# A graph network kernel: the weighted identities of rounds k = 1 to 4 made by ScalarE instead of VectorE

## The chip, the cores and the metric

The kernel runs on one core of a Trainium2 chip. The metric is the device time of one launch in microseconds (us), of which three runs are given as a median. The engines are called PE (TensorE, the matrix engine), DVE (VectorE), ACT (ScalarE), POOL (GpSimd) and SP (SyncE, which only issues transfers here).

## The reference

Four graph blocks follow one another on a table x of 50,000 nodes by 128 features, with 25,000 edges sorted by their target (dst). Each block's result is added to x and the sum is layer-normalised. All the change's work lies in the second block (L1):

```python
def prop(z):
    return jax.ops.segment_sum(edge_weight[:, None] * z[src], dst, num_segments=N_SUP)
for i in range(L):                       # L = 5 layers
    z = h @ W[i] + b[i]
    x_start = prop(z)
    xi = h
    for _ in range(RHP):                 # RHP = 5 rounds
        xi = (prop(xi) + x_start) / (2.0 + GAMA)
    mean = jnp.mean(xi, axis=0)
    var = jnp.var(xi, axis=0)
    out = gamma[i] * (xi - mean) / jnp.sqrt(var + BN_EPS) + beta[i]
    h = jnp.where(out > 0, out, LEAKY_SLOPE * out)
return h[seg_ids]
```

`prop` gathers the row of each edge's source, multiplies it by the edge's weight and adds up the rows that have one target. In this network all seg_ids are 0, so h is the same row everywhere before the first layer.

## The kernel before, in words

**Layout.** The 25,000 edges lie in T = 200 tiles of 125 edges (TE). A tile occupies 128 partitions. GR = 4 tiles are a group, so a round has GPR = 50 groups. Tables of edge rows live in HBM (`tabs`, three of them); a round reads one and writes another.

**Layers and rounds.** Layer l = 0 of block L1 is done in closed form (`scalars_*`). Layers l = 1 to 4 are a hardware loop, and in each of them the rounds k = 0 to 4 are written out (NL = 5), so k = 1 to 4 occur 16 times in all, with 800 groups. A round on each engine:

- POOL, `l1_gather` (line 1018): 200 indirect transfers, one per tile, each of 128 rows of 128 floats into ring G of 20 tiles (five groups). Before the first it waits until all stores of the round before have landed (`l_tab`), and before every second group until PE has read an old group (`l_ft`).
- PE, `forward` (line 1347, k >= 1): for each tile the matmul of the gathered tile with a diagonal matrix, the identity scaled by the tile's 128 edge weights. That turns the tile to features x edges and weights it in one step, into a PSUM bank (`FT_`). It waits for the scan two groups back (`l_sc`), for the four diagonal matrices (`l_dg`), and for each tile's landing (`l_got`). `backward` (line 1372) turns a scanned group back to edges x features. PE runs forward of group n+1, then backward of group n (`lagged`).
- DVE, `scanned` (line 1410): the running sum along the edges, cut where the target changes (`keyrow` is 0 there); it reads PSUM and `keyrow`. Behind it `scaled_identity` (line 1382) makes the four diagonal matrices of the next group, as one product of 128 x 512 elements of `ident` and `wz` (both in SBUF) into a half of M. In k = 1 to 3 `rows_out` (line 1434) then adds the constant part and writes Y. In k = 4 (`last`) two other instructions follow the diagonal matrices: a masked product (line 1422, of `keyrow` and the scan, both in SBUF) and batch statistics (line 1425).
- ACT has nothing in k = 1 to 3. In k = 4 `kept_act` copies the scan of a group (`copied`, line 1326), then the turned-back rows of the group before it from PSUM to Y (`rows_out`, line 1333). In k = 0 it has two activations a group (lines 1313 and 1317).
- SP stores Y of each group to the table (line 995).

The order on each engine is written out by hand; semaphores (counts that start at 2 by `credit`, so that `g + 1` means "group g - 2 is done" and `g + 3` means "group g is done") tie the engines together. M has two halves of four matrices, `h = q % 2`, so the matrices of group n overwrite those of group n - 2. In `lagged` the first function runs one group ahead of the second.

```python
            if k:
                scaled_identity(0, 0)
            else:
                leaky_nodes(0, 0)
            lagged(dve, scanned, (lambda i, q: None) if last else rows_out)
```

Of the kernel before, what the change touches and what calls it, by code (L numbers as in the profile page):

```python
# [5 lines left out]
ALU, ACT, AX = mybir.AluOpType, mybir.ActivationFunctionType, mybir.AxisListType  # L6

P, D = 128, 128
# [3 lines left out]
GR = 4  # L12
# [5 lines left out]
NB = 10  # L18
# [3 lines left out]
NL = 5  # L22
# [13 lines left out]
def build(nc, x0, src, dst, ea, ew, w0, b0, w1, b1, gamma, beta, w2, b2, we, be, coef, linw, linb, asrc, adst, out):  # L36
# [31 lines left out]
    with ctx:  # L68
# [20 lines left out]
        ident = sb("ident", [P, P])  # L89
# [15 lines left out]
        wz = sb("wz", [P, TP])  # L105
# [11 lines left out]
        M = sb("M", [P, U, P])  # L117
# [39 lines left out]
        def steady(eng, *values):  # L157


            for v in values:  # L160
                if not isinstance(v, int):
                    eng.lower_val(v)
            eng.wait_ge(s_go, 1)
# [787 lines left out]
        def every_group(eng):  # L951

            with eng.Fori(0, NI) as i:
                for q in range(NB):
                    yield i, q

        def lagged(eng, one, two):

            one(0, 0)
            with eng.Fori(0, NI - 1) as i:  # L960
                for q in range(NB):
                    one(i + (q + 1) // NB, (q + 1) % NB)
                    two(i, q)
            for q in range(NB):
                if q < NB - 1:
                    one(NI - 1, q + 1)
                two(NI - 1, q)

        def group_no(l, k, i, q):

            return round_of(l, k) * GPR + NB * i + q
# [5 lines left out]
        def is_last(i, q):  # L977

            return isinstance(i, int) and i == NI - 1 and q == NB - 1
# [322 lines left out]
        def scalars_act(act):  # L1302
            for g in range(GPR):
                act.wait_ge(o_ex, g + 1)
                nc.scalar.copy(zt_at(GR * g), bank(g % 2)).then_inc(l_xc, 1)

        def turned_act(act, l):

            for i, q in every_group(act):
                h, n, g = q % 2, (l - 1) * GPR + NB * i + q, group_no(l, 0, i, q)  # L1310
                steady(act, n + 1, g + 3, g + 1)
                act.wait_ge(l_z, n + 1)
                nc.scalar.activation(HTR[h][:].rearrange("p s f -> p (s f)"), zt_at((NB * i + q) * GR), ACT.Identity,
                                     bias=tcol[:, 0:1], scale=scol[:, 0:1]).then_inc(l_hc, 1)
                act.wait_ge(l_ft, g + 3)
                act.wait_ge(l_sc, g + 1)
                nc.scalar.activation(M[:, GR * h:GR * h + GR, :], PS[:, FT_[h], :, :], ACT.Identity,  # L1317
                                     bias=tcol[:, 0:1], scale=scol[:, 0:1]).then_inc(l_he, 1)

        def kept_act(act, l):  # L1320

            def copied(i, q):
                g = group_no(l, NL - 1, i, q)
                steady(act, g + 3)
                act.wait_ge(l_sc, g + 3)
                nc.scalar.copy(zt_at((NB * i + q) * GR), S[q % 2]).then_inc(l_zc, 1)  # L1326

            def rows_out(i, q):
                g, before = group_no(l, NL - 1, i, q), 16 * stores_before(l, NL - 1, i, q)
                steady(act, g + 3, before)  # L1330
                act.wait_ge(l_bk, g + 3)
                act.wait_ge(l_tab[q % NG], before)
                nc.scalar.copy(group_of(Y, q % NG), PS[:, BK_[q % 2], :, :]).then_inc(l_ev, 1)
            lagged(act, copied, rows_out)

        def l1_pe(pe, l, k):

# [38 lines left out]
        def l1_dve(dve, l, k):  # L1376
            last = k == NL - 1

            def scaled_identity(i, q):
                h = q % 2  # L1380
                dve.wait_ge(l_ft, group_no(l, k, i, q) + 1)
                nc.vector.tensor_tensor(M[:, GR * h:GR * h + GR, :], ident[:].unsqueeze(1).to_broadcast([P, GR, P]),  # L1382
                                        wz[:, bass.ds((NB * i + q) * GR, GR)].unsqueeze(2).to_broadcast([P, GR, P]),
                                        ALU.mult).then_inc(l_dg, 1)

            def leaky_nodes(i, q):
                u, n = HTR[q % 2][:].rearrange("p s f -> p (s f)"), (l - 1) * GPR + NB * i + q
                dve.wait_ge(l_hc, n + 1)
                nc.vector.scalar_tensor_tensor(u, u, 0.01, u, ALU.mult, ALU.max).then_inc(l_hl, 1)

            def scanned(i, q):
                h, g, tile = q % 2, group_no(l, k, i, q), (NB * i + q) * GR
                n = (l - 1) * GPR + NB * i + q
                half = M[:, GR * h:GR * h + GR, :].rearrange("p s f -> p (s f)")
                if k == 0:
                    dve.wait_ge(l_he, n + 1)
                    nc.vector.scalar_tensor_tensor(half, half, 0.01, half, ALU.mult, ALU.max).then_inc(l_lr, 1)
                    if not is_last(i, q):
                        leaky_nodes(i + (q + 1) // NB, (q + 1) % NB)
                    dve.wait_ge(l_lr, n + 1)  # L1400
                    dve.wait_ge(l_wc[q % NG], 32 * (NB // NG * NI * (l - 1) + NB // NG * i + q // NG + 1))
                    nc.vector.tensor_tensor(half, half, WR[:, q % NG, :], ALU.mult).then_inc(l_mu, 1)
                    dve.wait_ge(l_mu, n + 1)
                else:
                    dve.wait_ge(l_ft, g + 3)
                dve.wait_ge(l_bk, g + 1)
                dve.wait_ge(l_sc, g + 2)
                if last:
                    dve.wait_ge(l_zc, n + 1)
                nc.vector.tensor_tensor_scan(S[h], keyrow[:, bass.ds(tile * P, GR * P)],  # L1410
                                             half if k == 0 else bank(FT_[h]), S[1 - h][:, GR * P - 1:GR * P],
                                             ALU.mult, ALU.add).then_inc(l_sc, 1)
                if k == 0:
                    dve.wait_ge(l_z, n + 3)
                    nc.vector.tensor_tensor(zt_at(tile).rearrange("p (s f) -> p s f", f=D), PS[:, ZB_[h], :, :],
                                            wide(bias, P, GR), ALU.add).then_inc(l_za, 1)
                elif not is_last(i, q):
                    scaled_identity(i + (q + 1) // NB, (q + 1) % NB)
                if last:
                    dve.wait_ge(l_sc, g + 3)  # L1420
                    mk = HTR[h][:].rearrange("p s f -> p (s f)")
                    nc.vector.scalar_tensor_tensor(mk, keyrow[:, bass.ds(tile * P + 1, GR * P)], 1.0, S[h],
                                                   ALU.subtract, ALU.mult).then_inc(l_mk, 1)
                    dve.wait_ge(l_mk, n + 1)
                    nc.vector.bn_stats(stL[:, bass.ds(NB * i + q, 1), :].rearrange("p a b -> p (a b)"),
                                       mk).then_inc(l_bn, 1)

            def rows_out(i, q):
                h, g = q % 2, group_no(l, k, i, q)
                dve.wait_ge(l_bk, g + 3)  # L1430
                if k == 0:
                    dve.wait_ge(l_za, (l - 1) * GPR + NB * i + q + 3)
                dve.wait_ge(l_tab[q % NG], 16 * stores_before(l, k, i, q))
                nc.vector.tensor_tensor(group_of(Y, q % NG), PS[:, BK_[h], :, :],  # L1434
                                        zt_at((NB * i + q) * GR).rearrange("p (s f) -> p s f", f=D),
                                        ALU.add).then_inc(l_ev, 1)

            if k:
                scaled_identity(0, 0)
            else:  # L1440
                leaky_nodes(0, 0)
            lagged(dve, scanned, (lambda i, q: None) if last else rows_out)

# [45 lines left out]
        with nc.Block() as block:  # L1489
# [89 lines left out]
            @block.scalar  # L1579
            def _(act):  # L1580
                def layer(l):
                    if isinstance(l, int):
                        scalars_act(act)
                        return
                    steady(act, NCOEF * l)
                    act.wait_ge(l_col, NCOEF * l)
                    turned_act(act, l)
                    kept_act(act, l)
                over_layers(act, layer)
                act.wait_ge(l_col, NCOEF * NL)  # L1590
                act.wait_ge(l_fin, 1)
                nc.scalar.activation(HT[:, 0, :], PS[:, ZB_[0], 0, :], ACT.Identity, bias=tcol[:, 0:1],
                                     scale=scol[:, 0:1]).then_inc(l_rb, 1)
# [824 lines left out]
```

## Time and profile before

| | us |
|---|---|
| runs shown | 9612.27 (median; 9603.39 to 9615.67) |
| the profiled execution, its own time | 9691.98 |
| its span in the profile | 9690.2 |
| POOL busy | 6759.2 (70%) |
| PE busy | 5711.1 (59%) |
| DVE busy | 5407.2 (56%) |
| ACT busy | 1448.9 (15%) |

How to read it: a busy share is an average over stages, and the kernel's stages have different limits. The stretch in which rounds k = 1 to 4 lie begins 2059 us after the span's start and ends at 7254 us. Within it the engines wait for each other group by group, so what counts is which of them sets the pace of a group. Instructions that only wait, branch, set registers or issue transfers are not busy time; of an indirect transfer on POOL the busy time is that of making it ready, not of moving the data. The granted share of PE's full clock is 0.627 over the execution.

### The profile page before, as it was taken

The page shows a single profiled execution, that of the slowest core. Times are in us where ns is not written, and L with a number is a line of the kernel's source. Part 1 is how long each engine was busy: PE and PEld are TensorE (multiplying, and loading weights), DVE is VectorE, ACT ScalarE, POOL GpSimd, SP SyncE. Part 2 cuts the span into 40 slices and gives each one's busy share as a digit, 9 for nine tenths or more (in the row PEclk, how much of TensorE's full clock was granted, in tenths as well). Part 3 has the DMA queues.
Part 4 walks back from the last instruction along what each step waited for, and adds up shares of the span by engine and source line. Part 5 has one row for each costly group of instructions (what it writes and reads, how often), then busy time and mean ns, then how long its engine had stood idle before and what let it go on. Part 6 is the DMA issues. An engine that isn't in the chain of part 4 may idle for free. (4 is left out here: it accounts for less than half of the span.)

```text
span 9690.2 us, 103316 instructions
## 1 busy us (share of the span) xinstructions
PE 5711.1 (59%) x24229; PEld 4276.2 (44%) x24229; DVE 5407.2 (56%) x12873; ACT 1448.9 (15%) x3028; POOL 6759.2 (70%) x6509
## 2 busy tenths in 40 slices
PE   4646557766666766666666666666661775630191
PEld 2436224544444544444545445544440664530170
DVE  5668764554445754456744457644457774530277
ACT  0115000210002200012200012100026113430006
POOL 4767663577777777777777777777776776767566
PEclk8765776775555855556855557755555888865555
DMA  3137101577555765656678656668766227961107
GB/s 144 43 101 245 25 3 36 118 111 99 98 98 103 132 104 98 98 98 112 124 99 101 99 97 124 113 98 96 99 99 232 63 68 149 183 115 28 20 31 323
DMA packets 564282, 1024.03 MB, mean 106 GB/s; under 512 B 192219, under 2 KB 275724, under 8 KB 563556
## 3 DMA queue, kind: packets, MB, share of 16 engines
q0 software_dynamic: 192032, 330.29, 32.3%
q1 hardware_dynamic: 354372, 588.76, 20.1%
q10 hardware_dynamic: 17664, 102.61, 2.6%
q8 instruction: 75, 1.23, 0.1%
q14 instruction: 139, 1.14, 0.0%
HBM read 561.87 MB, written 471.67 MB: 107 GB/s over the span
## 5 line engine op out<-in xcount | busy, mean ns | idle before, releaser
L1018 POOL DMA_INDIRECT G<-tab,gidx x4000 | 4050.6, 1013 | 1625.4 <-issue 1406.8
L1347 PE MATMUL PS<-M,G 128*128 128x128 f32 x6400 | 2073.2, 468 | 1524.1 <-DVE M L1382 1011.7
L1347 PEld LDWEIGHTS PS<-M,G 128*128 128x128 f32 x6400 | 1504.5, 314 | 2175.3 <-DVE M L1382 917.5
L1410 DVE TENSOR_TENSOR_SCAN UO<-keyrow,UT,PS 128x512 f32<-128x512 f32 (+1 forms) x400 | 511.9, 1280 | 1112.9 <-PE PS L1347 1112.9
L1410 DVE TENSOR_TENSOR_SCAN UT<-keyrow,UO,PS 128x512 f32<-128x512 f32 (+1 forms) x400 | 512.0, 1280 | 1030.7 <-PE PS L1347 1030.7
L1326 ACT COPY big<-UO 128x512 f32 (+1 forms) x100 | 61.8, 618 | 3666.0 <-DVE UO L1410 3666.0
L1434 DVE TENSOR_TENSOR Y<-PS,big 128x512 f32<-128x512 f32 x800 | 546.0, 683 | 12.8 <-PE PS L1372 7.0
L1105 POOL DMA_INDIRECT Y<-pair_d,G x400 | 402.4, 1006 | 200.0 <-issue 130.8
L1382 DVE TENSOR_TENSOR M<-ident,wz 128x512 f32<-128x512 f32 x800 | 534.3, 668 | 0.0
L758 ACT ACTIVATE big<-big,nb,rs 128x128 f32<-128x128 f32 x1173 | 461.3, 480 | 428.0 <-POOL nb L749 357.7
L1372 PE MATMUL PS<-ident,UT 128*128 128x128 f32 x1600 | 422.8, 420 | 8.3 <-DVE UT L1410 8.3
L1372 PE MATMUL PS<-ident,UO 128*128 128x128 f32 x1600 | 423.6, 420 | 0.0
L1350 PE MATMUL PS<-ident,G 128*128 128x128 f32 x800 | 195.1, 310 | 364.9 <-DMA G<-tab,gidx 315.8
L1372 PEld LDWEIGHTS PS<-ident,UT 128*128 128x128 f32 x1600 | 343.2, 228 | 14.7 <-DVE UT L1410 14.7
L1257 PE MATMUL PS<-big 128*128 128x400 f32 x800 | 322.2, 529 | 44.0 <-DVE G L1151 26.8
L1372 PEld LDWEIGHTS PS<-ident,UO 128*128 128x128 f32 x1600 | 347.4, 230 | 0.0
L450 POOL DMA_INDIRECT G<-in_x,ridx x200 | 208.8, 1044 | 156.9 <-DVE ridx L520 95.2
L2260 PE MATMUL PS<-ident,cf 128*100 128x128 f32 x8 | 2.0, 426 | 526.6 <-DVE cf L2206 526.6
L2304 POOL DMA_INDIRECT agg<-Y,sidx x200 | 197.5, 988 | 153.5 <-DVE Y L2355 105.1
L902 POOL DMA_INDIRECT gidx<-lastpos,src_i x200 | 231.3, 1157 | 103.0 <-issue 68.0
L1350 PEld LDWEIGHTS PS<-ident,G 128*128 128x128 f32 x800 | 109.3, 148 | 431.6 <-DMA G<-tab,gidx 380.1
L1317 ACT ACTIVATE M<-PS,tcol,scol 128x512 f32<-128x512 f32 x200 | 155.4, 777 | 843.3 <-PE PS L1350 843.3
(500 smaller groups left out, 11436.0 us busy)
## 6 DMA issues: line engine op xcount, KB each, us to landing
tab<-Y SPq DMA_DIRECT2D x1050, 256.0 KB, 3.2
big<-agg SPq DMA_DIRECT2D x90, 832.0 KB, 12.6
G<-tab,gidx POOLq DMA_INDIRECT x4000, 4.1
WR<-w_d SPq DMA_DIRECT2D x200, 256.0 KB
big<-x SPq DMA_DIRECT2D x60, 832.0 KB, 4.9
xt_d<-big SPq DMA_DIRECT2D x30, 858.0 KB, 19.2
x2n<-big ACTq DMA_DIRECT2D x30, 838.5 KB, 3.5
big<-x2n SPq DMA_DIRECT2D x30, 838.5 KB, 12.6
```

The source lines that it names most:

```text
L450: pool.indirect_dma_start(G[:, j, 0:D], None, x0, bass.IndirectOffsetOnAxis(ap=ridx[:, j:j + 1], axis=0)).then_inc(a_got[j], 16)
L758: ins = nc.scalar.activation(X[0:np_, j, 0:D], V[0:np_, j, :], ACT.Identity, scale=rs[0:np_, s, j:j + 1], bias=nb[0:np_, s, j:j + 1])
L902: pool.indirect_dma_start(gidx[:, t:t + 1], None, lastpos, bass.IndirectOffsetOnAxis(ap=src_i[:, t:t + 1], axis=0)).then_inc(g_got, 16)
L1018: pool.indirect_dma_start(G[:, t % RG, 0:D], None, tab_in(k), bass.IndirectOffsetOnAxis(ap=gidx[:, t:t + 1], axis=0)).then_inc(l_got[t % R ...
L1105: pool.indirect_dma_start(GS[:, t, :], None, pair_d, bass.IndirectOffsetOnAxis(ap=G2[:, t:t + 1], axis=0)).then_inc(o_got, 16)
L1257: ins = nc.tensor.matmul(bank2(n % 2)[:, j, :], OH[:, 2 * n + j, :], CT, start=True, stop=True)
L1347: ins = nc.tensor.matmul(PS[:, FT_[h], j, :], G[:, s, 0:D], M[:, GR * h + j, :], start=True, stop=True)
L1350: ins = nc.tensor.transpose(PS[:, FT_[h], j, :], G[:, s, 0:D], ident[:])
L1372: ins = nc.tensor.transpose(PS[:, BK_[h], j, :], UR[h][:, j, :], ident[:])
L1382: nc.vector.tensor_tensor(M[:, GR * h:GR * h + GR, :], ident[:].unsqueeze(1).to_broadcast([P, GR, P]), wz[:, bass.ds((NB * i + q) * GR, GR ...
L1410: nc.vector.tensor_tensor_scan(S[h], keyrow[:, bass.ds(tile * P, GR * P)], half if k == 0 else bank(FT_[h]), S[1 - h][:, GR * P - 1:GR * P ...
L1434: nc.vector.tensor_tensor(group_of(Y, q % NG), PS[:, BK_[h], :, :], zt_at((NB * i + q) * GR).rearrange("p (s f) -> p s f", f=D), ALU.add). ...
```

## The change

ACT gets a function `scaled_identity`: it waits until PE has read the half of M (`l_ft`) and until the scan of two groups before is done (`l_sc`), then makes the four diagonal matrices with four activations (Copy, with the tile's column of `wz` as scale), the last of which raises `l_dg`. In rounds k = 1 to 3 ACT runs this for every group and nothing else. In k = 4 it runs it one group ahead of `copied` and `rows_out`, which now come as a pair. DVE's product and its wait are gone.

```diff
+        def scaled_identity(act, l, k, i, q):
+            h, g = q % 2, group_no(l, k, i, q)
+            steady(act, g + 1)
+            act.wait_ge(l_ft, g + 1)
+            act.wait_ge(l_sc, g + 1)
+            for j in range(GR):
+                ins = nc.scalar.activation(M[:, GR * h + j, :], ident[:], ACT.Copy,
+                                           scale=wz[:, bass.ds((NB * i + q) * GR + j, 1)])
+            ins.then_inc(l_dg, 1)
+
+        def weighted_act(act, l, k):
+            for i, q in every_group(act):
+                scaled_identity(act, l, k, i, q)
...
-            lagged(act, copied, rows_out)
+
+            def behind(i, q):
+                copied(i, q)
+                rows_out(i, q)
+            lagged(act, lambda i, q: scaled_identity(act, l, NL - 1, i, q), behind)
...
-            def scaled_identity(i, q):
-                h = q % 2
-                dve.wait_ge(l_ft, group_no(l, k, i, q) + 1)
-                nc.vector.tensor_tensor(M[:, GR * h:GR * h + GR, :], ident[:].unsqueeze(1).to_broadcast([P, GR, P]),
-                                        wz[:, bass.ds((NB * i + q) * GR, GR)].unsqueeze(2).to_broadcast([P, GR, P]),
-                                        ALU.mult).then_inc(l_dg, 1)
...
-                elif not is_last(i, q):
-                    scaled_identity(i + (q + 1) // NB, (q + 1) % NB)
...
-            if k:
-                scaled_identity(0, 0)
-            else:
+            if k == 0:
                 leaky_nodes(0, 0)
...
                     turned_act(act, l)
+                    for k in range(1, NL - 1):
+                        weighted_act(act, l, k)
                     kept_act(act, l)
```

## Rows read from the trace of the kernel before

**Rows 1.** Waits, rounds 1 to 3 of layer 2: us in total, times, longest us.

```profile
POOL G L1018 <- issue: 177.4, 582, 0.3
POOL G L1018 <- DMA tab<-Y: 33.3, 3, 13.7
POOL G L1018 <- PE PS L1347: 4.6, 15, 0.3
...
PE PS L1347 <- DVE M L1382: 185.8, 147, 2.2
PE PS L1347 <- DMA G<-tab,gidx: 86.6, 151, 6.6
```

**Rows 2.** The gathers of rounds 1 to 3: window, length, POOL busy (instructions), clock, DMA share, GB/s.

```profile
2061.90:2320.00 258.10, 196.06 (x200) 0.51 0.85 97
...
sum 3094.30, POOL 2340.28; mean POOL 195.02
```

**Rows 3.** The same for the gathers of round 4 of the four layers.

```profile
2863.80:3128.00 264.20, 201.44 (x200) 0.51 0.56 97
...
sum 1056.00, POOL 805.38; mean POOL 201.34
```

**Rows 4.** Two groups of round 3, layer 2: start us, length us, instruction.

```profile
4011.91 1.28 DVE L1410 TENSOR_TENSOR_SCAN UT<-keyrow,UO,PS 128x512 f32<-128x512 f32 x1 [2.86 <-PE PS L1347]
4012.11 0.96 POOL L1018 DMA_INDIRECT G<-tab,gidx  x1 [0.30 <-issue]
4013.11 0.67 DVE L1382 TENSOR_TENSOR M<-ident,wz 128x512 f32<-128x512 f32 x1
4013.37 1.23 POOL L1018 DMA_INDIRECT G<-tab,gidx  x1 [0.30 <-issue]
...
4018.33 0.68 DVE L1434 TENSOR_TENSOR Y<-PS,big 128x512 f32<-128x512 f32 x1
...
4018.68 0.95 POOL L1018 DMA_INDIRECT G<-tab,gidx  x1 [0.30 <-issue]
```

**Rows 5.** A group of round 4, layer 2: start us, length us, instruction.

```profile
4330.46 0.80 PE L1347 MATMUL PS<-M,G 128*128 128x128 f32 x2 [0.64 <-DMA G<-tab,gidx]
...
4331.05 1.06 PE L1372 MATMUL PS<-ident,UO 128*128 128x128 f32 x4
...
4332.68 0.67 DVE L1382 TENSOR_TENSOR M<-ident,wz 128x512 f32<-128x512 f32 x1
4332.96 0.62 ACT L1326 COPY big<-UT 128x512 f32 x1 [4.13 <-DVE UT L1410]
...
4333.40 1.65 PE L1347 MATMUL PS<-M,G 128*128 128x128 f32 x6 [1.29 <-DVE M L1382]
4333.48 0.58 ACT L1333 COPY Y<-PS 128x512 f32<-128x512 f32 x1
...
4338.06 0.68 DVE L1422 SCALAR_TENSOR_TENSOR OT<-keyrow,UO 128x512 f32<-128x512 f32 x1
...
4338.26 1.31 POOL L1018 DMA_INDIRECT G<-tab,gidx  x1 [0.30 <-issue]
```

**Rows 6.** The gathers and the products of line 1382: duration ns min/median/max.

```profile
L1018 POOL DMA_INDIRECT G<-tab,gidx x4000: 938/952/1879, 1760.3 to 7244.1; - x191
...
L1382 DVE TENSOR_TENSOR M<-ident,wz x800: 665/668/731, 2059.1 to 7246.0; 128x512 f32<-128x512 f32 x160
```

**Rows 7.** ACT by line and shape: count, busy us, mean ns of one.

```profile
L758 ACT ACTIVATE big<-big,nb,rs 128x128 f32<-128x128 f32 x1170 | 459.8, 480 | 425.9 <-POOL nb L749 357.7 <-DVE nb L779 26.1 <-issue 18.7
...
L2044 ACT COPY UO<-PS 128x128 f32<-128x128 f32 x30 | 8.0, 266 | 47.8 <-PE PS L2118 47.8
```

**Rows 8.** ACT's sequencer at line 1326: duration ns min/median/max.

```profile
L1326 ACTq FUSED_REGOPS  x160: 61/64/64, 2878.4 to 7202.8; - x160
```

**Rows 9.** The end of round 3, layer 2: backward and `rows_out` of its last group.

```profile
4228.99 1.11 PE L1372 MATMUL PS<-ident,UT 128*128 128x128 f32 x4 [0.52 <-DVE UT L1410]
...
4230.14 0.69 DVE L1434 TENSOR_TENSOR Y<-PS,big 128x512 f32<-128x512 f32 x1 [0.62 <-PE PS L1372]
```

## The prediction, as it stands on record

> **What bounds the kernel now.** I read three views in turn. The waits of POOL in rounds k = 1 to 3 say that it waits for nobody between gathers [rows 1]: 582 of its pauses are "issue", at 177.4 / 582 = 0.305 us each, only 15 are for PE (4.6 us in three rounds), and the only long ones are the three handovers to the next round. So in these rounds POOL is the engine that sets the pace: a gather's own time plus 0.30 us, four times a group. The windows give that time: 2340.28 us for 2400 gathers, 0.975 each [rows 2]. In round 4 it is 805.38 us for 800, 1.007 each [rows 3], a pace of 4 x (1.007 + 0.30) = 5.23 us a group.
>
> PE waits 185.8 us in these three rounds for the matrices M, which looks like the prize, and 86.6 us for gathers [rows 1]. It is none: a group's four tiles come at POOL's pace, and with M there sooner PE waits for the tiles instead.
>
> The third view is the timeline, and it shows why a gather costs more than the 0.95 that most of them take. The gather at 4013.37 began 0.26 us into DVE's product of line 1382, when 0.41 of it was left, and took 1.23. The one at 4018.68 began inside `rows_out` (line 1434), the one at 4012.11 inside the scan, and they took 0.95 and 0.96 [rows 4]. The scan and `rows_out` read one operand from PSUM, the product reads both from SBUF. In round 4 the masked product (line 1422), both operands in SBUF, does the same: a gather begun inside it took 1.31 [rows 5]. So **a DVE instruction with two SBUF inputs holds back a gather that begins inside it**. DVE itself is off the path: it waited 2.86 us for PE before that scan [rows 4].
>
> **The change part by part.**
>
> *Product gone, k = 1 to 3.* I take 0.948 for a gather that nothing holds up: the median of all 4000, held ones among them, is 0.952, the least 0.938 [rows 6], and most rows print 0.95. With 0.952 the next figure would be 55. 2340.28 - 2400 x 0.948 = 65 us are then stretch [rows 2], 65 / 12 = 5.4 us a round, and no other DVE instruction there has two SBUF inputs; the 800 products take 0.67 each, 0.73 at most [rows 6], so they are not held up in turn. POOL sets the pace, so all of it comes back: **-65 us**. As a check: a gather starts every 1.257 us, and one started with r us of the product left is late by about r - 0.13 (0.41 left, 0.28 late), which over a product of 0.67 us and any phase is 0.54 x 0.54 / 2 / 1.257 = 0.12 us a group, 6 us a round.
>
> *Product gone, k = 4.* The stretch is 805.38 - 800 x 0.948 = 47 us, 11.8 a round [rows 3], from the product and line 1422 together. Line 1422 stays, and moves up by 0.6 us to where the product stood, right behind the scan. There a two-input instruction costs 5.4 us a round, as in k = 1 to 3. So 47 - 4 x 5.4 = 25: **-25 us**. Bounds: 0.13 a group more or less from its phase; if line 1422 lost nothing at its new place, -47; if three quarters of the 47 are its own and stay, -12.
>
> *DVE's 0.67 us a group themselves* are worth nothing: after them DVE waits for PE, which waits for the gathers. At a round's end no product stands between the last group's scan, its backward and its `rows_out` [rows 9]: the last group issues none, by the code. So the handover stays as it is.
>
> *Four activations a group, k = 1 to 3.* The trace has no copy with one pointer operand. From below: a 128x128 COPY from PSUM takes 0.266 [rows 7]; 128x512 ones take 0.04 more from SBUF than from PSUM (0.62 and 0.58) [rows 5], so 0.30. From above: the ACTIVATE of line 758, 128x128 from SBUF with two pointers (scale and bias), takes 0.48, and 1170 of them in 459.8 us are 0.393 apart, so neighbours overlap by 0.09. I take the middle, 0.39, as this one has a single pointer: x = 3 x 0.30 + 0.39 = **1.29 us a group**, between 0.93 and 1.66. They can start when the scan two groups back is done, 1.4 us after that group's forward, and are needed when the forward one group on has ended, 5.1 us after it: some 3.7 us, on an engine that has nothing else. Cost zero; the cover would be gone only above that. Sequencer time, one register instruction of 0.064 each [rows 8], fits under an activation. Of transfers the change moves none.
>
> *Four activations a group, k = 4.* Here the order matters: ACT makes the matrices of group n+2 only after `rows_out` of group n, which waits for backward n, which stands on PE behind forward n+1. That closes a ring that was not there before: end of forward to end of backward 0.85 (4331.26 to 4332.11), to `rows_out` 0.05 (4230.10 to 4230.14) [rows 5, 9], its copy 0.58 less 0.10 of overlap (the copy before it starts 0.52 before it and lasts 0.62), the four activations x, to forward 0.05, and forward's eight passes: six take 1.65, two 0.80, so eight 2.08. Together 3.51 + x = **4.80 us**, against POOL's pace afterwards of 5.11 (5.23 less 25 / 200). It stays under it; cost zero, with 0.31 us a group in hand. `copied` moves behind the activations, but the scan that waits for it is two groups on.
>
> **Sum**: -65 - 25 = -90 us. The profiled execution has 9691.98 us, so 9602 for its like; it is 0.8% above the median run, and I carry the difference over unscaled: 9612.27 - 90 = **9522 us**.
>
> *A page's rule against the row.* The gather held up in the row was late by less than what was left of the product. The Trainium skill, page "SBUF — State Buffer", section "A bandwidth-pool intuition that's wrong (but worth ruling out)", has such a transfer blocked until the DVE instruction ends plus about 115 ns. By that rule each of 50 x 0.67 / 1.257 = 27 gathers a round would lose 0.335 + 0.115 on average, 12 us a round, and the change would give 16 x 12 = 192 us. The busy sums hold only 65 + 47, so the measurement decides.
>
> **The rivals.**
>
> *A. Round 4 turns onto ScalarE's ring (faster, but less).* With x above 1.60 the ring is longer than 5.11, and each 0.1 us costs 50 x 4 x 0.1 = 20 us. At the upper bound of 1.66 that is 12 us: 9534. At x = 1.92 (four at 0.48, no overlap) 64 us: 9586. For it: without overlap four of 0.39 take 1.56, right below the threshold. Against: line 758 shows the overlap [rows 7].
>
> *B. The same mechanism far enough to be slower.* It needs x above 2.145 to pass +19 us. One place: the activations of k = 4. If each takes the two-pointer price without overlap and its register instruction is not hidden, x = 4 x (0.48 + 0.064) = 2.18, the ring is 5.69, and -90 + 200 x (5.69 - 5.11) = +26: 9638. Of this the trace shows only the single prices. The Trainium skill, page "ScalarE: Activation LUTs", section "Rules for kernel authors", says to use VectorE, not ScalarE, for a multiplication; 1.29 against 0.67 us here agrees on the price, and whether it matters is what the ring decides.
>
> *C. No change.* The stretch would not come back: something else takes up POOL's 65 + 25 us, for instance the landings, for which PE waits 86.6 us [rows 1], because the gathers run at the memory's pace rather than POOL's. 9612. Against it: POOL's pauses are "issue" and not a full ring, and the transfer engines are 0.85 busy in one window shown and 0.56 in the other [rows 2, 3], with the gather's own time no longer in the first. That the change doesn't do what it says I exclude: nothing on DVE makes M afterwards.
>
> *D. The page's rule above*, 9420: no chance, since the sums bound it.
>
> **How the numbers follow.** A measurement of this kernel can tell some 0.2%, 19 us. Forecast 0.75; A at 9534 to 9590 0.08; C 0.10; B 0.07. Faster is 0.82 (forecast and nearly all of A), same 0.11, slower 0.07. The range: below, the whole stretch of both kinds gone, -112, gives 9500; above, the forecast's weak end (-55 by the floor of 0.952, -12 in round 4) is 9545, and I go on to 9590 to hold A and some of what lies toward C.
>
> **What would show it.** Right: the gathers' busy time in the windows of k = 1 to 3 falls to 190 us a round, with none above 1.0 us; in k = 4 to some 195, with the stretched ones all inside line 1422; ACT's four at 1.2 to 1.4 us a group; the pause for "issue" unchanged; PE's waits move from M to the gathers. Wrong: gathers still stretched where no two-SBUF instruction runs (C), or PE in k = 4 waiting for ACT's M and POOL for PE (A, B).

## The result, and the profile after

| | before | after |
|---|---|---|
| median of five runs, us | 9609.03 | 9562.54 |
| lowest and highest | 9603.39, 9615.67 | 9557.24, 9568.96 |
| the profiled execution, its own time | 9691.98 | 9559.96 |

The ratio is 0.9953 (95% interval 0.9942 to 0.9964): 46 us faster, where 90 were forecast. The sign and the range held; the size is half.

The busy times of the page after, and its costliest groups that the change touches:

```profile
PE 5802.3 (61%) x24229; PEld 4310.9 (45%) x24229; DVE 4949.1 (52%) x12073; ACT 2449.6 (26%) x6228; POOL 6656.3 (70%) x6509
...
L1018 POOL DMA_INDIRECT G<-tab,gidx x4000 | 3952.7, 988 | 1622.0 <-issue 1407.3
L1365 PE MATMUL PS<-M,G 128*128 128x128 f32 x6400 | 2226.2, 472 | 1344.2 <-DMA G<-tab,gidx 949.2
...
L1313 ACT ACTIVATE M<-ident,wz 128x128 f32<-128x128 f32 x3200 | 1021.4, 390 | 2382.4 <-DVE UO L1421 1238.9
```

The product's 534 us are gone from DVE, which waits longer for PE instead, and ACT's four activations a group take 1021 us. In k = 1 to 3 PE's waits moved from M to the gathers, as forecast. In k = 4 they did not: PE waits for M in nearly every group, now for ACT's. That is half of the forecast's sign of rival A. The other half, POOL waiting for PE, is absent (k = 4 of layer 2: us in total, times, longest us):

```profile
PE PS L1365 <- ACT M L1313: 93.4, 48, 2.2
...
POOL G L1018 <- PE PS L1365: 1.5, 5, 0.3
```

The windows of the gathers after, k = 1 to 3, answer to [rows 2] (first, last and sum of twelve):

```profile
2056.20:2314.00 257.80, 190.23 (x200) 0.52 0.82 100
...
6628.00:6884.00 256.00, 188.72 (x200) 0.51 0.63 101
sum 3081.50, POOL 2275.41; mean POOL 189.62
```

And k = 4, to [rows 3]:

```profile
2840.60:3100.00 259.40, 195.42 (x200) 0.53 0.50 99
...
sum 1035.20, POOL 779.18; mean POOL 194.80
```

2340.28 to 2275.41 is the forecast's 65 us to the microsecond, and 805.38 to 779.18 is 26 where 25 were forecast. Counted gather by gather, those begun inside the product lost 64.5 us in k = 1 to 3 of the kernel before, which is the whole stretch there; in the changed kernel no gather of k = 1 to 3 takes over 0.97 us, and all 78 stretched ones of k = 4 began inside the masked product.

Yet these 91 us of POOL time appeared as 46 in the timed runs. The two profiled executions, on the other hand, lie 132 us apart. Some 28 of those fall between the last rounds and the third scatter (indirect transfers to `agg`, one per tile), where the two kernels are the same: 1165 and 1137 us from the last transfer of the second scatter to the first of the third. So the profile of before was not an execution like the timed ones. That is the question that the experiments take up.

### The profile page after: what moved, and what is told of

The parts are those of the page before. It is cut to its first block and busy times, and to the rows that moved or that the text cites. A ratio compares the mean times of both kernels' runs of the same rounds, so it can differ in the third digit from the quotient of the medians.

```text
span 9558.2 us, 109668 instructions
## 1 busy us (share of the span) xinstructions
PE 5802.3 (61%) x24229; PEld 4310.9 (45%) x24229; DVE 4949.1 (52%) x12073; ACT 2449.6 (26%) x6228; POOL 6656.3 (70%) x6509
## 5 line engine op out<-in xcount | busy, mean ns | idle before, releaser
L1018 POOL DMA_INDIRECT G<-tab,gidx x4000 | 3952.7, 988 | 1622.0 <-issue 1407.3
L1365 PE MATMUL PS<-M,G 128*128 128x128 f32 x6400 | 2226.2, 472 | 1344.2 <-DMA G<-tab,gidx 949.2
L1365 PEld LDWEIGHTS PS<-M,G 128*128 128x128 f32 x6400 | 1539.3, 310 | 2052.8 <-DMA G<-tab,gidx 1463.8
L1313 ACT ACTIVATE M<-ident,wz 128x128 f32<-128x128 f32 x3200 | 1021.4, 390 | 2382.4 <-DVE UO L1421 1238.9
L1384 PE MATMUL PS<-cf 128*128 128x512 f32 x400 | 260.9, 741 | 8.3 <-DVE UT L1421 4.2
```

Source lines behind the costliest of these rows:

```text
L1018: pool.indirect_dma_start(G[:, t % RG, 0:D], None, tab_in(k), bass.IndirectOffsetOnAxis(ap=gidx[:, t:t + 1], axis=0)).then_inc(l_got[t % R ...
L1313: ins = nc.scalar.activation(M[:, GR * h + j, :], ident[:], ACT.Copy, scale=wz[:, bass.ds((NB * i + q) * GR + j, 1)])
L1365: ins = nc.tensor.matmul(PS[:, FT_[h], j, :], G[:, s, 0:D], M[:, GR * h + j, :], start=True, stop=True)
L1384: nc.tensor.matmul(bank(BK_[h]), QR[:, q % NG, :], BD, start=True, stop=False)
```

## The experiments

The runs were made in three jobs, and the record names another chip for each of them (9, 12 and 14). The kernel before ran in each as well, and its median differed: 9580.77, 9606.91 and 9687.95 us, so every figure below is read against its own job. It was profiled in job 1 only. "This chip" in an expectation written for job 2 means the chip of job 1, whose profiles it was worked out from.

| run | median us | ratio to before (95%) |
|---|---|---|
| job 1: before again | 9574.65 | 0.9993 (0.9984 to 1.0001) |
| ACT in k = 1 to 3 only | 9570.38 | 1.0001 (0.9979 to 1.0023) |
| identity in PSUM, product on DVE | 9561.89 | 0.9978 (0.9969 to 0.9987) |
| after again | 9542.95 | 0.9959 (0.9946 to 0.9972) |
| job 2: after, a spare product on DVE | 9621.35 | 1.0015 (1.0006 to 1.0024) |
| ACT in k = 4 only | 9581.27 | 0.9976 (0.9966 to 0.9985) |
| before, product 0.5 us later | 9794.91 | 1.0191 (1.0177 to 1.0205) |
| after, scan of k = 0 from PSUM | 9537.46 | 0.9927 (0.9914 to 0.9941) |
| job 3: after, ACT's part of k = 4 doubled | 9837.31 | 1.0142 (1.0123 to 1.0160) |
| after again | 9691.36 | 1.0002 (0.9992 to 1.0011) |
| after, scan of k = 0 from PSUM | 9689.70 | 1.0000 (0.9991 to 1.0010) |
| the same, masked product from PSUM too | 9719.86 | 1.0029 (1.0018 to 1.0041) |

### Before and after, profiled again in one job

No edit.

> The kernel before, unchanged, profiled again beside its own timed runs. The page that the forecast rested on was of an execution of 9692 us, while the timed runs have 9609. Theory (the stretch is in every execution, and the missing half of the gain is lost elsewhere): the gathers of k = 1 to 3 are busy 195 us a round again and those of k = 4 201 us, and the ratio is 1.000. Rival (that execution was a slow one, and its stretch was larger than the usual): the new profile has a span of about 9610 us, and the gathers' busy time is lower, so that the sum over the 16 rounds exceeds that of the changed kernel by about 50 us instead of 90.

> The changed kernel again, in the same job as the others. Both theories: 9562 within 5 us, ratio 0.995, gathers of k = 1 to 3 at 189.6 us a round with none above 1.0 us. It gives the profile that stands beside that of the kernel before from the same chip.

The changed kernel's ratio came as expected (0.9959), its median not (9543 for 9562), as the whole job was faster.

The windows of the gathers in k = 1 to 3 of layers 1 and 2, for the kernel before in this job (k = 1 of each layer, and the sum of the six; columns as in [rows 2]):

```profile
2058.90:2317.00 258.10, 192.74 (x200) 0.51 0.54 100
...
3419.20:3677.00 257.80, 192.84 (x200) 0.51 0.51 100
...
sum 1546.60, POOL 1153.54; mean POOL 192.26
```

And for the changed one (k = 2 of layer 1, and the sum):

```profile
2322.10:2580.00 257.90, 190.73 (x200) 0.50 0.54 101
...
sum 1545.30, POOL 1146.14; mean POOL 191.02
```

The rival was right: here the kernel before loses little to the stretch. Summed over all layers its gathers are busy 2301 us in k = 1 to 3 and 803 in k = 4, the changed kernel's 2281 and 779. That is 20 + 24 = 44 us, against 38 measured. The landings differ too. This is the time from issue to landing in k = 2 of layer 1 (min/median/max), first in the execution that the forecast used, then in this job's kernel before:

```profile
DMA to landing us min/median/max: 2.9/3.8/4.9
```

```profile
DMA to landing us min/median/max: 2.9/3.5/4.5
```

Over the whole kernel, for the gathers whose landing the trace shows, it is 4.1 us at the median and 13.4 at most in the forecast's execution, 3.5 and 7.2 here. What sets the stretch is the phase, that is, where the product stands against the gathers. Of the 600 products of k = 1 to 3, 18% here had a gather begin in their first 0.55 us, against 45% in the forecast's execution, about what a random phase gives (0.55 / 1.257 = 44%). A group's scan, and the product behind it, come after the landing of its last tile, so later or more scattered landings can move that phase. How much is due to which is argued and not shown: in the round above the landings are hardly more scattered, only 0.3 us later, and yet 23 of its 50 products met a gather in their first 0.55 us, against 12 of 50 here.

In k = 4 the masked product, one product later, meets the gathers in either case. It also carries most of the gain there: in this job it held gathers back by 36 us before and 18 after, while the product itself had cost 7. So 18 of the 25 us that k = 4 gave come from the masked product's new place right behind the scan, and not from the absence of the other.

### The same product with one operand in PSUM

```diff
-                nc.vector.tensor_tensor(M[:, GR * h:GR * h + GR, :], ident[:].unsqueeze(1).to_broadcast([P, GR, P]),
+                nc.vector.tensor_tensor(M[:, GR * h:GR * h + GR, :], PS[:, 6, 0, :].unsqueeze(1).to_broadcast([P, GR, P]),
...
+                        link(dve, "dve", nc.vector.tensor_copy(PS[:, 6, 0, :], ident[:]))
```

> The kernel before with one edit: DVE's product reads the identity from PSUM instead of SBUF, everything else stays on DVE. Theory (the two SBUF inputs are the cause): no gather of k = 1 to 3 is stretched, busy 190 us a round, and the gain is that of the full change or a little more, 40 to 60 us, 9550 to 9570, although DVE still spends its time. Rival (it is DVE's time, or M being late for PE, that the change takes away): no gain, 9609, or a slight loss, as the product becomes a little longer.

The identity is copied into PSUM once. It gained 19 us, where 40 to 60 were expected. Two rows of its timeline, a product and a gather that begins inside it:

```profile
3769.22 0.67 DVE L1382 TENSOR_TENSOR M<-PS,wz 128x512 f32<-128x512 f32 x1
...
3769.57 0.95 POOL L1018 DMA_INDIRECT G<-tab,gidx  x1 [0.30 <-issue]
```

Nothing is held, DVE spends the same 0.67 us, and k = 1 to 3 show the same busy time as the full change (191.01 a round in its six windows). So it is the operands and not DVE's time. It stays 19 us behind the full change: in k = 4 the masked product keeps its late place and most of its stretch (791 us against 779 over the four layers), which explains 12 of them. The other 7 stay open.

### One part alone

```diff
-                    for k in range(1, NL - 1):
-                        weighted_act(act, l, k)
```

This is the edit, against the changed kernel, for ACT in k = 4 only; DVE's product is put back in k = 1 to 3, and ACT's first group of k = 4 waits for the last forward of k = 3. For ACT in k = 1 to 3 only, the reverse.

> ACT makes the matrices in k = 1 to 3 alone, DVE again in k = 4. Theory (two SBUF inputs hold back a gather begun inside; the gain is spread over the rounds as the stretch is, 65 and 25 of 90): three quarters of the measured gain of 46 us, so some 35 us, 9574. Rival (k = 4 costs time by its ring through ACT, which eats the gain of k = 1 to 3): this kernel is faster than the full change, 9540 or less.

> ACT makes the matrices in k = 4 alone, DVE in k = 1 to 3. Theory: the gain here is what k = 4 lost of its stretch, 803 to 779 us over the four layers, so 20 to 25 us: 9556 to 9561, more than the k = 1 to 3 part gave on this chip (769 + 767 + 764 to 760 each, 20 us). Rival (the ring through ACT costs what the stretch gives back): 9581, with PE in k = 4 waiting for M and POOL for PE.

k = 4 alone gave 26 us, as expected and more than half of the change, though it is a quarter of the rounds. k = 1 to 3 alone gave 10 at the median, under the 35 expected, and its interval is so wide that it holds both 20 us and a loss: inconclusive by itself. Two of its twelve runs lie apart, at 9690 and 12369 us; the other ten have a mean of 9569. What its profile says is that the gathers of k = 1 to 3 are free again (759 us each over four layers) while those of k = 4 are held (801). Neither shows the ring to cost anything.

The profile of the kernel with ACT in k = 4 only tells of the product in job 2, where the kernel before took 9607 us, nearly the 9609 of the first timed runs. Its gathers of k = 1 to 3 are busy 2304 us, 29 above the 2275 of unheld ones. With some 24 in k = 4 (781 us there, and 805 in the next run) that makes 53 us on paper, near the 46 measured at first.

### A product that nobody needs

The changed kernel, and DVE multiplies the same two SBUF operands again behind each scan of k = 1 to 4, into an unused PSUM bank. It waits only for the one before it.

```diff
...
+                    nc.vector.tensor_tensor(PS[:, 6, :, :], ident[:].unsqueeze(1).to_broadcast([P, GR, P]),
+                                            wz[:, bass.ds(tile, GR)].unsqueeze(2).to_broadcast([P, GR, P]),
+                                            ALU.mult).then_inc(l_dm, 1)
```

> The changed kernel, and DVE makes a product of the same two SBUF operands again behind each scan of k = 1 to 4, whose result nobody reads (into an unused PSUM bank). The matrices still come from ACT. Theory (two SBUF inputs hold back a gather that begins inside them, as often as the phase has it): the gathers of k = 1 to 3 are stretched again as in the kernel before on this chip (about 192 us a round instead of 190), in k = 4 about 201, and the gain of 38 us is gone: 9570 to 9585. Rival (the gain is that M is ready sooner for PE): it stays, 9545.

The gain is gone and 14 us more (1.0015). The gathers are busy 768, 772 and 767 us in k = 1 to 3, where this job's kernel with the product on DVE in these rounds has 767, 770 and 767; in k = 4 they are busy 805 (803 in the kernel before of job 1). The matrices came from ACT all the while, so M being ready sooner is not the gain. The 14 us are unexplained.

### The product half a microsecond later

The kernel before, with a memset of an unused PSUM bank ahead of each product.

```diff
...
+                    nc.vector.memset(bank(7), 0.0).then_inc(l_dm, 1)
                     scaled_identity(i + (q + 1) // NB, (q + 1) % NB)
```

> The kernel before, with a memset of an unused PSUM bank ahead of the product, about 0.5 us, so that the product stands 0.5 us later against the gathers. On this chip 18% of the products had a gather begin in their first 0.55 us and most had the next one 0.6 to 1.0 us after their start. Theory (the stretch is set by the phase between landing and issue, not by the product alone): the next gather now falls at 0.1 to 0.5 us, three quarters are held back by 0.2 us or more, the gathers of k = 1 to 3 are busy some 198 us a round instead of 192, and the kernel is 70 to 120 us slower than before: 9650 to 9700. Rival (DVE is off the path and the product costs what it costs wherever it stands): 9581.

188 us slower, twice what was expected. Two groups of its timeline, k = 3 of layer 2:

```profile
3976.99 0.48 DVE L1420 MEMSET PS<- 128x512 f32 x1
3977.38 0.67 DVE L1383 TENSOR_TENSOR M<-ident,wz 128x512 f32<-128x512 f32 x1
3977.39 1.49 POOL L1019 DMA_INDIRECT G<-tab,gidx  x1 [0.30 <-issue]
...
3981.70 2.01 POOL L1019 DMA_INDIRECT G<-tab,gidx  x1 [0.30 <-issue]
3981.82 0.48 DVE L1420 MEMSET PS<- 128x512 f32 x1
3982.22 0.67 DVE L1383 TENSOR_TENSOR M<-ident,wz 128x512 f32<-128x512 f32 x1
```

The first gather began with the product and lost 0.54, as expected. The second began before the memset and lost 1.06. Counted over the trace, gathers begun inside a product lost 116 us, against 26 in the kernel before of job 1: that is the phase, 90 us. Another 141 lie on gathers that began inside the memset or up to 0.17 us before it, so the memset was no neutral delay; the masked product, moved away, cost 28 less. The direction is the theory's, the size is mixed.

### How far round 4 is from ACT's ring

The changed kernel, and in k = 4 ACT makes four further activations of the same form ahead of the four that count.

```diff
+            if k == NL - 1:
...
+                for j in range(GR):
+                    ins = nc.scalar.activation(PS[:, 6, j, :], ident[:], ACT.Copy,
+                                               scale=wz[:, bass.ds((NB * i + q) * GR + j, 1)])
+                ins.then_inc(l_dm, 1)
```

> The changed kernel, and ACT runs four further activations of the same form in k = 4 ahead of the four that make the matrices (their result goes to an unused PSUM bank). Theory (k = 4 has a ring of 3.51 us plus ACT's activations, against POOL's pace of about 5.1): ACT's part grows from 1.28 to about 2.5, the ring to 6.0, and k = 4 is paced by it: 200 groups x 0.9 us, so 160 to 190 us slower than the changed kernel, 9710 to 9750 where that has 9560; POOL then waits for PE. Rival (POOL sets the pace in k = 4 whatever ACT does): no more than 10 us.

In the changed kernel (job 1) a group of k = 4 looks like this:

```profile
4211.94 0.80 PE L1365 MATMUL PS<-M,G 128*128 128x128 f32 x2 [0.31 <-DMA G<-tab,gidx]
4212.53 1.06 PE L1390 MATMUL PS<-ident,UO 128*128 128x128 f32 x4
...
4213.67 0.59 ACT L1347 COPY Y<-PS 128x512 f32<-128x512 f32 x1 [3.38 <-PE PS L1390]
...
4214.15 1.28 ACT L1313 ACTIVATE M<-ident,wz 128x128 f32<-128x128 f32 x4
...
4215.48 0.80 PE L1365 MATMUL PS<-M,G 128*128 128x128 f32 x2 [1.89 <-ACT M L1313]
```

From the end of forward at 4212.74 to the next forward at 4215.48 are 2.74 us, and with forward's 2.08 (the forecast's figure) that makes 4.82: the ring of the forecast was 4.80. The median from one forward's end to the next is 4.97 in k = 4, the average 5.12, close to POOL's 5.11. With ACT's part doubled:

```profile
4341.56 0.59 ACT L1356 COPY Y<-PS 128x512 f32<-128x512 f32 x1 [2.55 <-issue]
4342.05 1.24 ACT L1318 ACTIVATE PS<-ident,wz 128x128 f32<-128x128 f32 x4
...
4343.23 1.26 ACT L1322 ACTIVATE M<-ident,wz 128x128 f32<-128x128 f32 x4
...
4344.54 1.71 PE L1374 MATMUL PS<-M,G 128*128 128x128 f32 x8 [3.06 <-ACT M L1322]
```

ACT's part is 2.44, the median pace of k = 4 becomes 5.99 (6.0 expected), POOL's pauses there grow by 90 us, and the kernel is 146 us slower than the changed one of its job; 160 to 190 were expected, from a base whose own pace there was 5.10 at the median but 5.18 on average. The ring is real, and the change stays some 0.3 us under POOL's pace of 5.1.

### The change where landings are slow

No edit: the changed kernel in job 3.

> The changed kernel again, as the base of the other three of this job. 0.995 to 0.996 of the kernel before.

This missed: no gain at all. Here the kernel before has 9688 us, like the profiled execution behind the forecast (9692). The stretch from the second to the third scatter, the same in both kernels, is alike too: 1156 us here and 1165 there, where job 1 has 1120 and 1124. Job 3's gathers, changed kernel (windows of k = 1 to 3 of layer 1):

```profile
2059.80:2317.00 257.20, 189.73 (x200) 0.51 0.89 96
2329.60:2587.00 257.40, 190.21 (x200) 0.51 0.91 96
2601.40:2859.00 257.60, 190.18 (x200) 0.50 0.90 97
```

The landings in k = 2 of layer 1, and POOL's waits there:

```profile
DMA to landing us min/median/max: 2.9/12.0/18.2
```

```profile
POOL G L1018 <- issue: 58.5, 190, 0.7
POOL G L1018 <- DMA tab<-Y: 12.1, 1, 12.1
POOL G L1018 <- PE PS L1365: 8.1, 9, 2.0
```

No gather is stretched in these rounds, as in job 1. But the transfer engines are 0.9 busy instead of 0.5 (job 1), a landing takes 12 us at the median, up to 18, and POOL waits for PE to free the ring. PE's forwards end 5.19 to 5.24 us apart on average in k = 1 to 3, where job 1 has 5.03 and the kernel before in the forecast's execution 5.14 to 5.18. Against job 1 the rounds k = 1 to 3 are 100 us longer over the four layers, and none of it is gather time: half is POOL waiting for a free place in the ring, half is the handover at the end of each round (14 us instead of 10), which waits for the last landings and stores. So here the landings set the pace. What POOL does not lose to the stretch goes into a longer row of transfers under way. That is rival C, by its mechanism.

One link is argued and not shown. The kernel before was not profiled in job 3, so that it loses the 65 us of stretch there is taken from the forecast's execution. Why the same transfers land slower in one job than in another no run shows either; the jobs ran on different chips, and chip and time can't be told apart.

### Two further operands moved to PSUM

The changed kernel, and in k = 0 the weighted half goes to a PSUM bank, from where the scan reads it.

```diff
-                    nc.vector.tensor_tensor(half, half, WR[:, q % NG, :], ALU.mult).then_inc(l_mu, 1)
+                    nc.vector.tensor_tensor(bank(6 + h), half, WR[:, q % NG, :], ALU.mult).then_inc(l_mu, 1)
...
-                                             half if k == 0 else bank(FT_[h]),
+                                             bank(6 + h) if k == 0 else bank(FT_[h]),
```

> The changed kernel, and in k = 0 the weighted half goes to a free PSUM bank, so that the scan of k = 0 reads one operand from PSUM instead of two from SBUF. In the profile of the changed kernel the gathers begun inside that scan carry 104 us of the stretch of k = 0 (192 gathers, 1.49 us on average). Theory: they come down to 0.95, the busy time of k = 0 falls from 910 us over four layers to about 810, and the kernel is 80 to 100 us faster than the changed one: 9445 to 9465. Rival (k = 0 is paced by DVE, whose instructions there fill most of a group): the busy time falls, but waits take its place, and less than 30 us come back.

> The kernel whose scan of k = 0 reads PSUM, again, now beside the changed kernel in one job: 20 to 35 us under it. In its first run the gathers of k = 0 were 109 us less busy than the changed kernel's, yet the rounds k = 0 became only 37 us shorter, so what is left there is not POOL's pace.

Job 2 had it 69 us under the kernel before, the best of this study (0.9927). The changed kernel was not in that job. The gathers of k = 0 in that run:

```profile
1760.90:2050.00 289.10, 200.79 (x200) 0.89 0.86 137
...
sum 1157.00, POOL 800.95; mean POOL 200.24
```

Job 1's changed kernel has 910 there. But from the first gather of k = 0 to that of k = 1 it is only 37 us less over the four layers (1205 in job 1, 1168 here), so both sides were half right: the stretch goes, and something else holds what is left. DVE's instructions, some 4.7 us a group and more with waits, are one candidate. The landings are another: in k = 0 their median went from 4.2 us in job 1 to 9.9 here. No run separates the two. In job 3 it gave 2 us over the changed kernel, where 20 to 35 were expected and a run can differ by more, which fits landings that had the pace there.

With the masked product of k = 4 reading a second copy that ACT makes in PSUM:

```diff
+                nc.scalar.copy(bank(6 + q % 2), S[q % 2]).then_inc(l_c2, 1)
...
-                    nc.vector.scalar_tensor_tensor(mk, keyrow[:, bass.ds(tile * P + 1, GR * P)], 1.0, S[h],
+                    dve.wait_ge(l_c2, n + 1)
+                    nc.vector.scalar_tensor_tensor(mk, keyrow[:, bass.ds(tile * P + 1, GR * P)], 1.0, bank(6 + h),
```

> The same, and in k = 4 ACT copies the scan a second time, into a free PSUM bank, so that the masked product has one operand from PSUM. Theory: no DVE instruction of k = 1 to 4 has two SBUF inputs any more, the gathers of k = 4 fall from 779 to 759 us over the four layers with none above 1.0 us, and the kernel is 15 to 20 us under the one without it. Rival (the second copy lies in ACT's ring, 3.51 + 1.28 + 0.5 = 5.3 us a group): it is slower by up to 40 us, with POOL waiting for PE in k = 4.

The theory's part on POOL held: the gathers of k = 4 fell to 758.5 us over the four layers. The kernel was 28 us slower than the changed one all the same, and 30 slower than the one it builds on. The groups of gathers, this kernel and the changed one of the job:

```profile
L1019 POOL DMA_INDIRECT G<-tab,gidx x4000 | 3832.3, 958 | 1855.9 <-issue 1425.8 <-DMA tab<-Y 283.4 <-PE PS L1367 101.7
```

```profile
L1018 POOL DMA_INDIRECT G<-tab,gidx x4000 | 3961.2, 990 | 1721.7 <-issue 1402.3 <-DMA tab<-Y 227.1 <-PE PS L1365 83.4
```

POOL saved 129 us in the gathers and spent 134 more waiting: 56 for the stores of a round before it can begin the next, 18 for PE, and 24 under "issue" are named in the rows. The kernel with only the scan of k = 0 changed waits 281.2 us for stores too, so that part is not k = 4's.

The trace does place the loss. From the first gather of k = 4 to the end of the layer's statistics it is 1094 us over the four layers, against 1064 in the changed kernel of this job and 1073 in the one it builds on, while k = 1 to 3 agree within 2 us and k = 0 is 11 us shorter than in the changed kernel. So the loss lies in k = 4, and there PE's forwards end 5.28 us apart on average instead of 5.18, and POOL's pauses grow by some 15 us. That is what the expectation's rival said (a ring of 5.3 us, up to 40 us slower, POOL waiting for PE). But the landings in k = 4 also rose, from 4.0 to 9.9 us at the median, and no run separates the longer ring from them. In a job with fast landings it was not tried, so whether it helps there is open.

## Why the prediction was right, and where it was off

- **The mechanism** was right: a DVE instruction with two SBUF inputs holds a gather that begins inside it. One operand in PSUM removes it, a spare product brings it back. The stretch that the forecast set out to remove (65 and 25 us) did vanish from the gathers' busy time (65 and 26). In k = 4 the masked product cost 5.2 us a round at its new place, where 5.4 were forecast.
- **ACT's cost** was right: one activation 0.386 us, four in 1.28 (forecast 1.29), the ring of k = 4 4.82 (4.80). Rivals A and B did not happen; the doubled part shows that with x = 2.44 they would have. PE does wait for ACT's M in k = 4 (93 us in one round), but POOL does not wait for PE, so it costs nothing: the sign of rivals A and B needed both.
- **The handover** stayed as it was in job 1 (10 us a round in both kernels). In job 3 it is 14.
- **The step that failed** is the first term of the sum, "POOL sets the pace, so all of it comes back: -65 us", together with the line that carried the sum over to the median unscaled. The stretch was read from one execution that was 0.8% slower than the median, and what sets that execution apart bears on the term itself. In it the products met the gathers as often as a random phase would have it (45%; the check with any phase confirmed just this execution), and its landings were later. In job 1, with prompt landings, k = 1 to 3 lose 20 us and not 65; with k = 4's 24 the change is worth 44 on paper and 38 in the timed runs. In job 2 it is 29 and some 24 on paper. In job 3, with slow landings, nothing comes back (1.0002), because the landings set the pace. The first five timed runs lie near the first two cases: 46. No profile exists of a kernel before among these first timed runs, so for them this is inferred from the other jobs. That k = 4 came out at 24 in job 1 as well is luck in part: the forecast's execution has it as 13 us of product and 13 of masked product, job 1 as 7 and 18.
- **Rival C** had the right mechanism for job 3, and a chance of 0.10. I had set it aside because POOL's pauses were "issue" and its own time did not grow at a transfer share of 0.85. A share of 0.85 was a warning and not a proof: the changed kernel of the first profile has 0.82 in a window without extra pauses, and in job 3, at 0.9 and landings of 12 us, POOL waits.

## What to carry to other kernels

Where POOL makes ready indirect transfers back to back, look at each DVE instruction's operands: two in SBUF, and here a transfer that began inside was late by what was left of it less 0.13 us, and one operand in PSUM or another engine ended it. How much it costs depends on the phase between the two engines, so take the sum from an execution whose time is that of the timed runs, and if it is not, find out first why. Before counting time won on the issuing engine, check the landings and the transfer share: an engine that issues faster than its transfers land only makes a longer queue, as in job 3. An instruction that moves because another is gone can be worth more than the one that is gone, as the masked product was in k = 4.

## What the runs showed of the hardware that I had not expected

- A memset of 128x512 float32 into PSUM (0.48 us, no SBUF operand) held back a gather that was already under way: begun 0.12 us before it, the gather took 2.01 us instead of 0.95. It ended 0.82 us after the product behind the memset, just as one begun inside that product does (0.83 after it for the 1.49 us gather above). A two-SBUF product alone never did that to a gather begun ahead of it: in the forecast's execution none of those begun inside the scan, whose end the product follows, took over 0.97. A memset with no such product behind it was not tried.
- The same kernel had medians of 9581, 9607, 9609 and 9688 us in four jobs, with the runs of a job within 35 us of each other. The difference goes with the landing time of the gathers (for the changed kernel 3.7 us at the median in the fastest job, 6.0 in the slowest), and the stretch between the second and third scatter, which no run here touches, shows it too (1119 to 1129 us in job 1, 1135 to 1139 in job 2, 1156 to 1165 in job 3).
